# Norms moved across stage ends, a filter computation behind its neighbour, and the keys' rotation on VectorE, in a four-block vision tower

## The reference

```python
def _layernorm(x, axis=-1, eps=1e-05):
    m = jnp.mean(x, axis=axis, keepdims=True)
    v = jnp.var(x, axis=axis, keepdims=True)
    return (x - m) / jnp.sqrt(v + eps)
...
    h = h + _L0_attn_ref(_layernorm(h, axis=-1), L0_attn_qkv_w, ...)   # 12 heads of 16, q and k RMS-normed per head
    h = h + _L0_ffn_ref(_layernorm(h, axis=-1), ...)                   # causal rotary attention (12 query, 3 key heads of 64), then 16 experts, top 2
    h = h + _L1_attn_ref(_layernorm(h, axis=-1), ...)                  # state-space filter: a convolution with a computed response K
    h = h + _L1_ffn_ref(_layernorm(h, axis=-1), ...)                   # 4-bit quantised MLP with Gelu
    h = h + _L2_attn_ref(_layernorm(h, axis=-1), ...)
    h = h + _L2_ffn_ref(_layernorm(h, axis=-1), ...)                   # patch MLP, and expert pairs on 6 class positions
    h = h + _L3_attn_ref(_layernorm(h, axis=-1), ...)                  # attention mixed with a state-overlap attention
    h = h + _L3_ffn_ref(_layernorm(h, axis=-1), ...)                   # 4 experts, top 1
```

## Time and profile before

| | |
|---|---|
| median of 3 runs | 1006.73 us (1000.97 to 1015.85) |
| the profiled execution's own time | 1011.79 us |
| its span | 1010.0 us, 17256 instructions |
| mean granted TensorE clock | 0.932 of full speed |
| busy: PE / DVE / ACT / POOL | 875.4 / 435.7 / 390.3 / 186.7 us |

### The profile page before, as it was taken

How to read it: one execution, slowest core, us unless ns; L and a number is a source line. 1 busy time by engine, 2 the same in 40 slices (tenths; PEclk the granted TensorE clock), 3 DMA queues, 4 the chain that set the end, 5 groups by cost and what they waited for, 6 DMA issues and landing times. The chain is left out here.

```text
span 1010.0 us, 17256 instructions
## 1 busy us (share of the span) xinstructions
PE 875.4 (87%) x6176; PEld 621.2 (62%) x6177; DVE 435.7 (43%) x914; ACT 390.3 (39%) x862; POOL 186.7 (18%) x223
## 2 busy tenths in 40 slices
PE   7879878999996359999989778998998899885997
PEld 5556656666764137777668356675677566663676
DVE  3266676775743202222238476562003566621011
ACT  2336663443432012222324564453251555411332
POOL 3450002443500512222300002320000000003012
PEclk9779999998998669999999799999999999987899
DMA  9700000000005981111132007301000211102111
GB/s 299 190 1 1 1 2 0 1 2 1 1 1 132 287 231 47 47 47 47 40 108 54 1 1 196 88 1 27 1 1 1 59 49 48 49 5 82 46 49 32
DMA packets 39388, 57.46 MB, mean 57 GB/s; under 512 B 4052, under 2 KB 32900, under 8 KB 39320
## 3 DMA queue, kind: packets, MB, share of 16 engines
q1 hardware_dynamic: 27800, 41.63, 15.1%
q10 hardware_dynamic: 8016, 7.20, 2.7%
q0 software_dynamic: 3504, 7.69, 2.2%
HBM read 43.28 MB, written 13.23 MB: 56 GB/s over the span
## 5 line engine op out<-in xcount | busy, mean ns | idle before, releaser
L78 PE MATMUL banks<-con 128*128 128x512 f32 (+1 forms) x188 | 90.6, 600 | 14.4 <-POOLq L1937 14.4
L1777 PE MATMUL banks<-moe_wu,moe_xf 96*128 x256 | 91.6, 503 | 1.3 <-issue 0.8
L603 PE MATMUL banks<-x,a_wqkv 96*96 96x272 f32 x288 | 78.0, 412 | 5.6 <-PEq L84 5.6
L1777 PEld LDWEIGHTS banks<-moe_wu,moe_xf 96*128 96x128 f32 x256 | 47.3, 194 | 31.2 <-issue 4.4
L603 PEld LDWEIGHTS banks<-x,a_wqkv 96*96 96x96 f32 x288 | 47.6, 172 | 24.6 <-issue 11.0
L78 PEld LDWEIGHTS banks<-con 128*128 128x128 f32 x188 | 37.0, 208 | 41.8 <-issue 38.3
L902 ACT ACTIVATE a_vt<-banks 102x384 f32<-102x384 f32 x96 | 42.3, 488 | 47.9 <-PE banks L680 47.0
L142 ACT ACTIVATE ln_sq<-x 96x544 f32<-96x544 f32 x32 | 21.0, 656 | 96.5 <-DVE x L134 96.4
L680 PE MATMUL banks<-con,a_vx 96*102 96x96 f32 x384 | 45.4, 263 | 8.5 <-ACT a_vt L902 5.5
L1944 POOL DMA_INDIRECT y_rows<-moe_ys,moe_back x32 | 30.7, 959 | 117.4 <-DVE moe_part L2038 112.4
L680 PEld LDWEIGHTS banks<-con,a_vx 96*102 96x102 f32 x384 | 34.8, 135 | 17.5 <-ACT a_vt L902 10.3
(11 more groups left out here) (387 smaller groups left out, 1792.3 us busy)
## 6 DMA issues: line engine op xcount, KB each, us to landing
moe_wu<-in_moe_up SPq DMA_DIRECT2D x16, 576.0 KB, 13.0
f_w<-in_f_e SPq DMA_DIRECT2D x10, 576.0 KB, 14.3
moe_wd<-in_moe_down SPq DMA_DIRECT2D x16, 288.0 KB, 14.0
moe_x_slots<-slots_zeros SPq DMA_DIRECT2D x1, 3104.0 KB, 25.0
moe_xs<-moe_x_slots ACTq DMA_DIRECT2D x32, 97.0 KB, 1.9
patch_px<-in_patches SPq DMA_DIRECT2D x4, 768.0 KB, 9.4
f_wu<-in_f_up SPq DMA_DIRECT2D x4, 582.0 KB
f_x_slots<-slots_zeros SPq DMA_DIRECT2D x1, 2310.0 KB, 32.7
```

The source lines that it names most:

```text
L78: self.nc.tensor.matmul(self.ps[bank][:, 0:width], self.ident, self.con[:, 0:width], start=True, stop=True)
L603: last = nc.tensor.matmul(ps[2 + m][0:HD, 0:CW], wqkv[:, a, j * D + m * HD:j * D + (m + 1) * HD], chunk(x, c)[:, a], start=a == 0, stop=a ...
L1777: last = nc.tensor.matmul(ps[2 + 2 * p + u][:, 0:BW], xf[0:KU[a], p, a], wu[0:KU[a], bass.ds(e, 1), a, u * BW:(u + 1) * BW].rearrange("p e ...
```

## The change

1. `Norm.var` waits only for an earlier chunk that shares its PSUM bank. Embedding gets banks (1, 2, 3, 1), s1 (1, 4, 5, 6); a0 gives its carried norm mean bank 1 and variance bank 5.
2. Embedding leaves its last norm to a0, and ends with two idle products. In a0 its mean stands behind the keys' projection, its variance behind the queries', its square, rstd and scale among ScalarE's and VectorE's first steps.
3. Part 1 of the response waits in a0 for both value expansions of chunk 0 (`v_spread`).
4. In g0, for chunks 1 to 3, the three key tiles are multiplied by the cosine on VectorE (from SBUF), and tile 3's swap and tile 2's turn stand ahead of `normalise(2c+1)`.
5. s1 makes all four norms, interleaved with the turning of weights; f1 carries none. f1 adds an idle product of 256 columns behind each of its first six up products.
6. f2 makes all four norms (4 idle products at its end in place of 3, and 2 more between); a3 carries none, and does the states first, their norm steps between the first projections.

```diff
     def var(self, pe, c):
         pe.wait_ge(self.squared, c + 1)
-        if c > 0:
-            pe.wait_ge(self.log_var, c)
+        for v in range(c - 1, -1, -1):
+            if self.var_banks[v] == self.var_banks[c]:
+                pe.wait_ge(self.log_var, v + 1)
+                break
...
-            ln.mean(pe, NC - 1)
             ln.var(pe, NC - 2)
-            ln.var(pe, NC - 1)
+            env.idle_products(2, 0)
...
             pe.wait_ge(w_in, 16)
+            if quantum:
+                pe.wait_ge(wo_in, 32)
+                states()
             project_k(0)
             for c in carried:
                 before.mean(pe, c)
+            if quantum:
+                env.idle_products(1, 4)
+                state_norms()
             project_q(0)
...
             for m in range(2):
                 project_v(0, m)
-            if quantum:
-                pe.wait_ge(wo_in, 32)
-                states()
-                env.idle_products(1, 4)
-                state_norms()
...
+            if quantum:
+                take_states()
             for t in range(2):
                 take(0, t)
+                if quantum:
+                    take_norms(t)
             if rms:
+                before.square(act, L)
                 take(0, 2)
                 head_rms(0)
                 take(0, 3)
                 head_rms(1)
+                before.rstd(act, L)
...
             if response is not None:
+                pool.wait_ge(v_spread, 2)
                 response.on_pool(pool, 1)
...
+            for c in carried:
+                before.centre(dve, c)
             if rms:
                 for t in range(2):
                     head_scale(0, t)
-            for c in carried:
-                before.centre(dve, c)
...
             if quantum:
-                for c in carried:
-                    before.scale(dve, c)
+                scale_states()
             spread_values(0)
...
-                    if c > 0:
+                    if 0 < c and t < JQ:
                         nc.gpsimd.tensor_tensor(by_token(raw[:, r % RB]), by_token(raw[:, r % RB]), table(env.cos), ALU.mult).then_inc(cos_done, 1)
...
-                if c == 0:
+                if c == 0 or t >= JQ:
+                    turned_raw = raw[:, r % RB].rearrange("p (i n) -> p i n", n=N)
+                    src = ps[2 + t % 2][:, 0:CW].rearrange("p (i n) -> p i n", n=N) if c == 0 else turned_raw
                     dve.wait_ge(swapped, r + 1)
...
                     turn(c + 1, 1)
+                    swap(c + 1, 3)
+                    turn(c + 1, 2)
                 normalise(2 * c + 1)
                 if more:
-                    for t in range(3, TQK):
+                    for t in range(4, TQK):
...
             ln.mean(pe, 1)
-            for n in range(4):
+            for n in range(2):
+                turn_weights(n)
+            ln.mean(pe, 2)
+            for n in range(2, 4):
                 turn_weights(n)
             ln.var(pe, 1)
-            ln.mean(pe, 2)
+            ln.mean(pe, 3)
+            ln.var(pe, 2)
+            env.idle_products(1, 7)
+            ln.var(pe, 3)
             for n in range(4, len(turns)):
                 turn_weights(n)
-            ln.var(pe, 2)
-            env.idle_products(3, 3)
...
-            before.mean(pe, L)
             env.idle_products(2, 7)
-            up(0, 0)
-            up(0, 1)
-            before.var(pe, L)
-            env.idle_products(2, 7)
-            for f in range(2, NF):
+            for f in range(NF):
                 up(0, f)
+                env.idle_products(1, 7, 256)
...
             ln.var(pe, 0)
+            env.idle_products(1, 3)
+            ln.mean(pe, 2)
             ln.var(pe, 1)
-            env.idle_products(3, 3)
+            env.idle_products(1, 3)
+            ln.mean(pe, 3)
+            ln.var(pe, 2)
+            ln.var(pe, 3)
+            env.idle_products(4, 3)
```

More of the change, by code:

```diff
@@ L583, in stage_narrow_attention @@
         carried = range(before.kept, NC) if before is not None else ()
[L584 to L585 removed]
+        for c in carried:
+            before.mean_bank, before.var_banks[c] = (1, 5) if rms else (0, 0)
         block = ctx.enter_context(nc.Block())
@@ L622, in states @@
             def states():
-                pe.wait_ge(before.ready, NC)
                 for m in range(2):
@@ L1131, in _ @@
             if quantum:
-                for c in carried:
-                    before.scale(dve, c)
+                scale_states()
             spread_values(0)
-            if quantum:
-                scale_states()
-            else:
-                for c in carried:
-                    before.scale(dve, c)
+            for c in carried:
+                before.scale(dve, c)
             ob = gated_b[:, 1] if quantum else cols(env, name + "_ob")[0:HD, :]
@@ L2291, in _, with stage_quantised_ffn @@
             ln.scale(dve, 0)
+            ln.centre(dve, 2)
+            ln.centre(dve, 3)
             quantise(1)
-            ln.centre(dve, 2)
             ln.scale(dve, 1)
             ln.scale(dve, 2)
-        return ln
-def stage_quantised_ffn(env, name, weights, before):
+            ln.scale(dve, 3)
+def stage_quantised_ffn(env, name, weights):
     nc = env.nc
@@ L2399, in _ @@
             scale_x(0)
-            before.square(act, L)
             scale_x(1)
             bias_h(0)
-            before.rstd(act, L)
             for c in range(NC):
@@ L2784, in build @@
             n1.sq, n1.rs = env.sq2, env.rs2
-            last = stage_narrow_attention(env, "a0", a0, rms=True, response=response, left=1, first_rms=n1)
+            last = stage_narrow_attention(env, "a0", a0, rms=True, response=response, before=last, left=1, first_rms=n1)
             env.end_stage()
@@ L2809, in build @@
                 f3 = ExpertWeights(env, inner, "f3", of("f3"))
-                stage_narrow_attention(env, "a3", a3, quantum=True, before=last, ahead=[f3_router, f3])
+                stage_narrow_attention(env, "a3", a3, quantum=True, ahead=[f3_router, f3])
                 env.end_stage()
```

59 lines of the change are left out of this document (27 added, 32 removed).

## The result

The changed kernel takes 1001.11 us (median of 20 runs, 994.72 to 1011.0), the kernel before, run beside it, 1009.14 (20 runs, 1000.77 to 1015.85): a ratio of 0.9914, 95% interval 0.9886 to 0.9942. It is 0.9% faster where 2.2% was forecast, and outside the range of 975 to 999. The profiled execution, 994.72, is the fastest of the 20 and flatters the change: it is 17.1 less than the profiled one of before.

A forecast was written before the change was run, and what follows sets the result against it. TensorE, busy 87% of the span, was taken to bound the kernel, the changed stages by chains through ScalarE, VectorE and GpSimd. Terms sum to 22.5, taken from a median of 1006.7: 984.2 us, range 975 to 999.

The forecast's parts named there:

- end of the embedding: At the embedding's end only chunk 2's norm ends the stage: 4.3 us earlier, between 3.3 and 4.5.
- start 5.4: From a0's start to the turning of values 17.5 us in place of 23.0: 5.4 gained, bounds 3.5 and 7.
- chunk 0 at 0: In a0's first chunk, up to 4.1 lost to GpSimd's response against about 4 from full clock: 0, bounds -3 and +3.
- s1: End of s1 4.6 us earlier, 0.6 left if the clock falls as before; 4.0 taken.
- f1: First Gelu 3.1 us sooner and 1.0 off f1's tail: 4.1 together, bounds 2 and 6.
- f2 and a3: f2 6.3 us longer, a3's start 4.5 shorter: a loss of 1.8, bounds 4 lost and 1 gained.
- g0, the clock: In g0, half of the 6 us the low clock costs in two rounds is won: 3, bounds 0 and 8.
- g0, the waits: In g0's three rounds, reordered key tiles win 0.4, 1.9 and 1.2: sum 3.5 us, bounds -1 and 5.8.
- The lock: In g0, VectorE instructions with two SBUF inputs and GpSimd SBUF reads exclude each other; without it 3 us more gained.
- Rival A: Low clock returns in g0, s1's end and a0's start: 13 us gained, 993.5, chance 0.22.
- B: GpSimd's response meets chunk 1's expansions, g0's rounds gain nothing, first transfer late, f2's end costs 4: 997 us, chance 0.11.
- C: In g0 `normalise` waits behind tile 3, clock falls mid-round, costing 26 against 16 from other terms: 1017 us, chance 0.05.

The follow-up runs named there:

- e10: e9 with three idle products of 256 columns before the scores of chunks 1 to 3 in g0: 983.95 us, ratio 0.9759.
- e13: Kernel before with four idle products of 256 columns before the scores of chunks 1 to 3 in g0, nothing else: 1006.01 us, ratio 0.992.
- e14: Changed kernel with three idle products before the scores of chunks 1 to 3 in g0, nothing else: 994.18 us, ratio 0.9843.
- e7: Changed kernel with tile 2's turn moved behind `normalise`, tile 3's swap still ahead: 998.98 us, ratio 0.9876.
- e9: Changed kernel without item 6, tile 2's turn behind `normalise`, GpSimd's response in two pieces: 990.76 us, ratio 0.984.
- e1: Kernel before with items 1 to 3 of the change alone: 1007.81 us, ratio 0.9947.
- e6: Changed kernel with item 6 undone (f2 and a3 as before): 993.1 us, ratio 0.9848.
- e15: e10 with two idle products of 256 columns before the first values are turned in a0 and a2: 987.46 us, ratio 0.9726.
- e4: Kernel before with item 6 of the change alone: 1016.56 us, ratio 1.0047.

## Why the prediction was wrong, step by step

Two steps of the prediction failed, and they carry most of the miss. It let a shortened wait of TensorE in g0 keep half of the clock's gain, and it set GpSimd's response against a full clock in a0's first chunk at 0. The runs showed that the clock falls behind the shortened waits as it did before, and that the first chunk got 3.0 longer (26.8 for 23.8, from the turning of values to chunk 1's scores).

With the table, each term can be held against the mean over the profiled executions with the old and the new code of a stage (a stage counts as new where nothing but this change is in it).

| term | forecast | old code | new code | measured |
|---|---|---|---|---|
| end of the embedding | 4.3 | 36.1 | 32.2 | 3.9 |
| a0 (start 5.4, chunk 0 at 0) | 5.4 | 117.6 | 115.1 | 2.5 |
| g0 (waits 3.5, clock 3.0) | 6.5 | 152.5 | 150.5 | 2.0 |
| s1 | 4.0 | 42.5 | 39.6 | 2.9 |
| f1 | 4.1 | 41.0 | 37.5 | 3.5 |
| f2 and a3 | -1.8 | 204.4 | 206.7 | -2.3 |
| sum | 22.5 | | | 12.5 |

12.5 lies between the two differences of medians, 8.0 and 13.6; stages the change leaves alone vary by as much as 4 between executions. The terms of f2 and a3 and of the embedding were right within 0.5, and the mechanism of s1 and f1 was.

- **g0, the clock: wrong.** "Of the clock's 6 I take half, 3." None came, and the step behind it failed: that the waits left would be under 1 us and might then keep the clock. They are 1.72, 1.36 and 1.72, and waits of 1.2 to 1.7 lower it like those of 1.9; only a filled wait keeps it (e10, e13, e14). The term itself was too small: the low clock cost 8, not 6. I had taken the second and third round alone, but in the first, too, the output projection took 7.32 for 5.74 in the kernel before:

```profile
209.93 7.32 PE L1360 MATMUL banks<-g_cx,g_wo 128*96 128x272 f32 x24
```

- **g0, the waits: mis-sized, 1.6 for 3.5** (1.9 where the fill keeps the clock in both, 142.7 for 144.6). The parts that I named for a key tile add to 1.8, and 1.7 was taken; it is 1.75 (227.23 to 228.98). The lock was right too: sine 0.98, turn 0.96. But I had the reduction held up in the first round alone. Counted from the scores of its group it starts 0.5 later in the second round and 1.4 later in the third as well, since only a turn and a swap lie between tile 2's own swap and its turn, too little for GpSimd's two products. So the rounds win 0.2, 1.3 and 0.1 in place of 0.4, 1.9 and 1.2. With the turn moved e7 and e9 win 1.4 of this back.
- **a0: start right, chunk 0 wrong.** The values are turned at 57.11 (forecast 56.9). "I put these against each other at 0": the collision cost 4.0, 2.5 of it as a wait and 1.5 by way of the clock (e9), and the gain of a full clock against it didn't come, since the clock fell at 59 to 60 in eight of the twelve profiles with the new start. In e1, e6, e14 and e15 it fell in chunk 0 only at 75 to 79; a0 has 113.8, 114.8 and 113.2 in the first three of them.
- **s1: 1.1 short, by its base.** The new stage is 39.6 as forecast. The low clock at the old one's end, taken as a fixed part of before, lasts 10 us there and about 3 in e4 and e13 (41.2 in place of 43.6). One profile was read as if it were the rule.
- **f1: 0.6 short.** First Gelu 3.6 after the start, 3.5 forecast. The tail's variance still waits 0.4, now for its square.
- **The base.** The median of three runs, 1006.7, was 2.4 under that of twenty.

Rival A (the low clock returns everywhere, 993.5) had the mechanism in g0, but not over a0's start nor at the end of s1, where the clock is full. B (the lock moves with the work, 997) had that of chunk 0, but the rotation won something and the first transfer came in time in all but one profile. Parts of both came true together, and I had priced them apart. C (1017) is out: `normalise` behind tile 3 cost 0.5 to 1.5 a round, and no g0 with the new order is longer than before.

**A version that beats both** is e10 (the change without item 6, tile 2's turn behind `normalise`, the response in two pieces, and g0's waits filled): 983.95 against 1010.92 for before on the same chip, 2.4% faster (2.0 to 2.8), where the changed kernel is 0.9% or 1.4% faster.

## What to carry to other kernels

Where a low clock follows a short wait of TensorE, fill the wait before you shorten it: three or four unread products (0.5 us each) in waits of 1.2 to 1.9 were worth 8 us of g0, and all the reordering around them 3. A fill pays only where the clock falls: in f1 it won 0.3, and in e15 the clock fell at the next wait instead. If you move work away from an engine it contends with, follow it to where it lands, and cut it into pieces that fit between the other engine's long operations. Sum a change against several profiles of before: where a stage's granted clock differs between executions, a term read from one of them is off by 2 to 4 us.
